# A smaller first transfer for the fold operands, and the first rounding of x moved from ScalarE to VectorE

## What is computed

```python
base = jnp.einsum('bsi,oi->bso', x, W)
low = jnp.einsum('bsi,bir->bsr', x, lora_A[labeler_index])
x = x + base + jnp.einsum('bsr,or->bso', low, lora_B_w) * 0.5
```

```python
y = irfft(rfft(x, n=1024) * rfft(K, n=1024))[..., :512] + x * D[:, None]
x = x + y * (arange(512) < length[:, None])
```

## Time and profile before

| | us |
|---|---|
| median of 3 executions | 196.37 |
| lowest and highest of them | 195.5 and 196.44 |
| the profiled execution | 195.38 |
| its span, first to last instruction | 193.3 |
| PE busy in the span | 188.3 (97%) |
| DVE, ACT, POOL busy | 125.5, 90.1, 69.9 |

### The profile page before, as it was taken

The page is one execution under the profiler, slowest core; times in us unless marked ns, Lnnn a source line. Parts: engine busy times, 40 slices in busy tenths (PEclk is TensorE's granted clock), DMA queues, the critical chain, the costliest instruction groups (busy, mean ns, idle before and its releaser), DMA issues.

```text
span 193.3 us, 2658 instructions
## 1 busy us (share of the span) xinstructions
PE 188.3 (97%) x937; PEld 157.7 (82%) x937; DVE 125.5 (65%) x163; ACT 90.1 (47%) x143; POOL 69.9 (36%) x111
## 2 busy tenths in 40 slices
PE   7799999999999999999999999999999999999994
PEld 3488887888888888888778888888999999999994
DVE  0699889369976067868006506379989777777743
ACT  2555075444339734334143221766566565565600
POOL 6048830000000377000000000279869867676700
PEclk9999999999999999999999999999999999999999
DMA  6989990000000000000001600045897988888634
GB/s 202 347 295 428 427 416 24 0 0 2 3 2 0 0 2 3 0 0 0 0 2 23 209 0 0 0 120 172 239 330 284 303 265 270 273 267 243 233 119 153
DMA packets 14654, 27.33 MB, mean 141 GB/s; under 512 B 2450, under 2 KB 4914, under 8 KB 13746
## 3 DMA queue, kind: packets, MB, share of 16 engines
q1 hardware_dynamic: 13922, 25.79, 39.0%
q10 hardware_dynamic: 720, 1.38, 2.0%
HBM read 18.69 MB, written 8.47 MB: 141 GB/s over the span
## 4 chain that ended last, share of the span: by engine, by line
PE 95%; DVE 2%; ACT 1%; issue 0%
PE y_ps L539 12%; PE y_ps L540 12%; PE y_ps L541 12%; PE k_ps L604 10%; PE k_ps L606 10%; PE k_ps L605 10%; PE low_ps L533 4%; PE low_ps L534 4%; PE low_ps L535 4%; PE y_ps L546 4%; PE y_ps L555 2%; PE y_ps L563 2%; PE y_ps L559 2%; PE low_ps L512 2%; PE k_ps L593 1%; PE k_ps L541 1%
## 5 line engine op out<-in xcount | busy, mean ns | idle before, releaser
L395 POOL TENSOR_TENSOR t_lo<-w_raw,t_hi 128x512 fp32r<-128x512 f32 x32 | 45.5, 1435 | 61.3 <-ACT t_hi L457 61.3
L741 DVE COPY_PREDICATED low_sel<-lab_mask,low_ps 32x512 f32<-32x512 int32 x32 | 23.3, 730 | 29.4 <-PE low_ps L535 28.4
L604 PE MATMUL k_ps<-xs_hi,t_hi 128*128 128x128 f32 (+3 forms) x130 | 41.6, 320 | 0.2 <-DVE x_all L813 0.2
L606 PE MATMUL k_ps<-xs_lo,t_hi 128*128 128x128 f32 (+3 forms) x130 | 41.7, 321 | 0.0
L605 PE MATMUL k_ps<-xs_hi,t_lo 128*128 128x128 f32 (+3 forms) x130 | 41.6, 320 | 0.0
L539 PE MATMUL y_ps<-x_hi,w_hi 128*128 128x512 f32 x104 | 40.6, 391 | 0.0
L541 PE MATMUL y_ps<-x_lo,w_hi 128*128 128x512 f32 x104 | 40.6, 391 | 0.0
L540 PE MATMUL y_ps<-x_hi,w_lo 128*128 128x512 f32 x104 | 40.6, 390 | 0.0
L753 DVE TENSOR_TENSOR xs_lo<-x_all,xs_hi 128x512 fp32r<-128x512 f32 x32 | 29.9, 938 | 4.7 <-ACT xs_hi L451 4.7
L813 DVE COPY_PREDICATED x_all<-len_mask,k_ps 128x512 f32<-128x512 int32 x31 | 23.2, 750 | 12.2 <-PE k_ps L606 11.9
L451 ACT CAST xs_hi<-x_all 128x512 fp32r<-128x512 f32 x32 | 19.9, 622 | 18.9 <-PE k_ps L606 18.8
(11 more groups left out here) (128 smaller groups left out, 218.7 us busy)
## 6 DMA issues: line engine op xcount, KB each, us to landing
w_raw<-k_pad SPq DMA_DIRECT2D x32, 256.0 KB, 4.3
out<-x_all SPq DMA_DIRECT2D x31, 256.0 KB, 3.6
x_all<-in_xt SPq DMA_DIRECT2D x7, 1024.0 KB, 13.9
w_raw<-in_wt ACTq DMA_DIRECT2D x4, 256.0 KB, 5.3
x_all<-in_xt SPq DMA_DIRECT2D x4, 256.0 KB, 7.4
ab_raw<-in_ab SPq DMA_DIRECT2D x1, 320.0 KB, 3.5
a_raw<-in_a_lab ACTq DMA_DIRECT2D x1, 320.0 KB, 7.2
out<-x_all SPq DMA_DIRECT2D x2, 128.0 KB, 1.7
```

Of the source, the lines that this page charges most:

```text
L395: g.tensor_tensor(t_lo[:, k % TR, :], t_raw[:, k % RAW, ::-1], f32(t_hi[:, k % TR, :]), ALU.subtract).then_inc(t_lo_done, 1)
L604: mm(o, t_hi[:, u, cols(lag)], xs_hi[:, b, x], start=(lag == 0), stop=False, skip_group_check=True)
L606: return mm(o, t_hi[:, u, cols(lag)], xs_lo[:, b, x], start=False, stop=ends, skip_group_check=True)
L741: v.copy_predicated(low_sel[:], lab_mask[rows, :].unsqueeze(1).to_broadcast([RANK, GH, P]), low_ps[rows, g % 2, :].rearrange("p (h b) -> p ...
```

## The change

- The transfer of `ab_raw` is cut in two. Rows 0 to 31 (A0 of chunk 0 and B beside it) go first; then chunk 0 of x; then rows 32 to 127; then chunks 1 to 3 of x. Each part has its semaphore.
- PE waits for the first part ahead of the first fold, and for the second part ahead of the second fold.
- The rounding of chunk 0 of x goes from ACT to DVE, between the two halves of the addition to W of chunk 0. It has a semaphore of its own (`x0_hi_done`), and the counts of `x_hi_done` are one less everywhere.
- ACT waits for both parts ahead of its use of B, much later.

```diff
-            sp.dma_start(ab_raw[:], ab).then_inc(ab_load, 16)
-            for c in range(CH):
+            sp.dma_start(ab_raw[0:RANK, :], ab[0:RANK, :]).then_inc(ab_load[0], 16)
+            sp.dma_start(x_all[:, 0:GH, cols(0)], xt[:, 0:GH, cols(0)]).then_inc(x0_load[0], 16)
+            sp.dma_start(ab_raw[RANK:P, :], ab[RANK:P, :]).then_inc(ab_load[1], 16)
+            for c in range(1, CH):
                 sp.dma_start(x_all[:, 0:GH, cols(c)], xt[:, 0:GH, cols(c)]).then_inc(x0_load[c], 16)
...
             def split_chunk_hi(c):
-                act.wait_ge(x0_load[c], 16)
-                s.copy(x_hi[:, 0:GH, cols(c)], x_all[:, 0:GH, cols(c)]).then_inc(x_hi_done, 1)
+
+                if c > 0:
+                    act.wait_ge(x0_load[c], 16)
+                    s.copy(x_hi[:, 0:GH, cols(c)], x_all[:, 0:GH, cols(c)]).then_inc(x_hi_done, 1)
...
-            act.wait_ge(ab_load, 16)
+            act.wait_ge(ab_load[0], 16)
+            act.wait_ge(ab_load[1], 16)
...
-            pe.wait_ge(ab_load, 16)
             for c in range(CH):
+                if c < 2:
+                    pe.wait_ge(ab_load[c], 16)
...
             def chunk(c):
-                pe.wait_ge(x_hi_done, c + 1)
+                if c == 0:
+                    pe.wait_ge(x0_hi_done, 1)
+                else:
+                    pe.wait_ge(x_hi_done, c)
...
-                for _, o in w_parts(c):
+                for n, o in w_parts(c):
                     v.scalar_tensor_tensor(w_raw[:, c, o], fold_ps[c][:, o], LORA_SCALING, w_raw[:, c, o],
                                            ALU.mult, ALU.add).then_inc(w_sum, 1)
-                dve.wait_ge(x_hi_done, c + 1)
+                    if n == 1:
+                        dve.wait_ge(x0_load[0], 16)
+                        v.tensor_copy(x_hi[:, 0:GH, cols(0)], x_all[:, 0:GH, cols(0)]).then_inc(x0_hi_done, 1)
+                if c == 0:
+                    dve.wait_ge(x0_hi_done, 1)
+                else:
+                    dve.wait_ge(x_hi_done, c)
```

More of the change, by code:

```diff
@@ L140, in conditioned_residual @@
         a_load = sem("a_load")
-        ab_load = sem("ab_load")
+        ab_load = [sem(f"ab_load{i}") for i in range(2)]
         idx_load = sem("idx_load")
@@ L161, in conditioned_residual @@
         masks = sem("masks")
+        x0_hi_done = sem("x0_hi_done")
         x_hi_done = sem("x_hi_done")
@@ L209, in buf_of, with hi_count, lo_count @@
             return slice(GH * (g % 2), GH * (g % 2) + GH)
-        def split_count(g):
+        def hi_count(g):
+            return CH - 1 + 2 * g
+        def lo_count(g):
             return CH + 2 * g
@@ L567, in low_group @@
             def low_group(g):
-                pe.wait_ge(x_hi_done, split_count(g))
-                pe.wait_ge(x_lo_done, split_count(g))
+                pe.wait_ge(x_hi_done, hi_count(g))
+                pe.wait_ge(x_lo_done, lo_count(g))
                 if g >= 2:
@@ L626, in _ @@
             pe.wait_ge(a_lo_done, 1)
-            pe.wait_ge(x_hi_done, CH)
+            pe.wait_ge(x_hi_done, CH - 1)
             pe.wait_ge(x_lo_done, CH)
@@ L727, in split_x_lo @@
             def split_x_lo(g, pair):
-                dve.wait_ge(x_hi_done, split_count(g - 1) + pair + 1)
+                dve.wait_ge(x_hi_done, hi_count(g - 1) + pair + 1)
                 b, h = GH * (g % 2) + 2 * pair, GH * g + 2 * pair
```

## The result

| | before | changed kernel |
|---|---|---|
| median of 6 executions, us | 196.28 | 199.09 |
| lowest and highest | 195.23 and 196.45 | 197.51 and 199.87 |
| the profiled execution, us | 195.38 | 199.87 |
| its span, us | 193.3 | 197.6 |

The medians are 2.8 us apart. The ratio on record is 1.0166, with a 95% interval of 1.0136 to 1.0196, which makes 2.7 to 3.8 us. I had forecast 0.4 us, with a range up to 197.8. The profiled execution is the slowest of the six, so its rows show more than the median loss.

What follows compares the result with a forecast made beforehand. PE was taken as the bound, busy 188.3 of 193.3 us. All terms were 0 or hidden except 0.4 us for rounding x on DVE, so the 196.37 us median became 196.8, range 195.6 to 197.8.

Steps and rivals of the forecast that it cites:

- What bounds the kernel: Whole kernel: PE, busy 188.3 of 193.3 us; the change aims at its 1.0 us wait ahead of chunk 0.
- The first part of ab alone: Start of the folds: an earlier landing hides behind PE's own queue; 0, at most 0.1 us gained.
- The first fold alone: Ahead of chunk 0: four folds run together, so one alone still ends at 6.58; 0, at most 0.1 us.
- The other three folds: Ahead of chunk 0: second part lands at 6.1, at most 6.6; folds take 1.0 us, hidden before 7.62.
- The rounding of x on DVE: Between DVE's two half sums of chunk 0: the new instruction costs 0.4 us, bounds 0.3 to 0.6.
- The tie at the low-rank product: Chunk 2's end: DVE's `a_lo` has about 0.1 us slack, so its delay makes PE lose 0.4 us.
- Rival A: Ahead of chunk 0: a late second part makes the folds hold PE; +1.5 us, 197.9 us; chance 0.10.
- Rival B: From the first fold on: PE's clock rises 2 to 3 us later; about +1.4 us, 197.8; chance 0.13.
- Rival C: Idle ahead of chunk 0: it delays the clock in timed executions; filling it gives 195.8 us; chance 0.12.
- Rival D: Start of the folds: ab's landing set it in timed executions; 0.5 us net gain, 195.9; chance 0.10.
- the sign given for D: DVE's first sum of chunk 0 starts clearly ahead of 6.5 us; also the sign for folds sharing the array.
- The number: Median of the changed kernel: likeliest 196.8 us, range 195.6 to 197.8.

Runs made afterwards that it cites:

- warm6: The kernel before with six instead of seven matmuls on the zeroed tile; 195.83 us, ratio 1.0.
- hole: The kernel before, transfers unchanged, with PE also waiting for chunk 0 of x ahead of the folds; 198.13 us, ratio 1.0119.
- x_then_whole: The kernel before with chunk 0 of x issued ahead of an uncut ab; 198.24 us, ratio 1.0154.
- cut_columns: As parts_in_row, but ab is cut by columns, each part with all 128 rows, and all folds wait for both; 196.73 us, ratio 1.0074.
- parts_in_row: The changed kernel with both parts of ab issued ahead of chunk 0 of x; 198.92 us, ratio 1.0146.
- x_on_dve: The kernel before with only the rounding of chunk 0 of x moved from ACT to DVE; 195.86 us, ratio 1.0006.
- transfers_only: The changed kernel's transfers and PE waits, with ACT rounding chunk 0 of x as in the kernel before; 199.06 us, ratio 1.018.
- filler: The changed kernel with eight matmuls on the zeroed tile between the first fold and the wait for ab's second part; 198.87 us, ratio 1.0173.
- hole_filled: As hole, with three matmuls on the zeroed tile ahead of PE's waits; 196.29 us, ratio 1.0027.
- halves: As parts_in_row, but ab is cut at row 64 and PE waits ahead of the first and third fold; 200.52 us, ratio 1.0259.
- folds_behind: The changed kernel with the folds of chunks 1 to 3 moved behind the first four matmuls of chunk 0; 198.11 us, ratio 1.015.

## Why the prediction was wrong, step by step

- **What bounds the kernel**: right. PE does, and the waits that matter are in the first 8 us.
- **The first part of ab alone, 0**: right. It landed at 3.2 us and was not waited for; warm6 shows that PE's own queue set 4.70.
- **The first fold alone, 0**: right. Alone and at the full clock it takes 1.12 us (4.33 to 5.45); in hole all four take 1.13 us (6.29 to 7.42).
- **The other three folds, "I take 6.1", bound 6.6, hidden**: this is the step that failed, a term of 0 in the sum. The part landed at 7.46, chunk 0 started 1.9 us late, and the clock added 2.3 us in the profiled execution. I had counted the bytes of SP's queue alone, while W's queue took more of the time than before, and held one more transfer worth 0.5 us at most. x_then_whole gives 6.40 for the same bytes uncut, and in cut_columns and parts_in_row one more transfer cost 1.0 us and the cut by rows another 1.2 for what is behind. The bound had come from no row on a transfer of fewer than 128 rows, and so was none. The price of the folds was short, too: a pass of 512 columns at the full clock starts 0.50 us after the one ahead of it (6.29 to 6.79 in hole's trace), not 0.43.
- **The rounding of x on DVE, c = 0.4**: the size was 0.33, within the bounds. The tie at the low-rank product is there (0.41 us idle in x_on_dve), and its cost in the median, 0.1 us (-0.4 to +0.6), leaves both 0 and 0.4 possible. In the changed kernel it is hidden altogether, since `a_lo` ends at 17.3 and the low-rank product comes near 20. Chunk 0 of x landed at 5.74, not at "about 5", just ahead of its use at 5.83.
- **Rival A, 0.10**: its mechanism is the one that happened, with the landing 0.1 us ahead of the 7.6 that it named, and a start at 9.51 instead of its 8.6. It was priced at the full clock, 1.0 us for three folds; they took 2.0.
- **Rival B, 0.13**: the clock was the other half, and its sign, starts 0.43 us apart behind 7.6, was met. Its reason stays open. In the profiled execution the clock was up ahead of the first fold, so that one can't test it; there the hole brought the clock down. In transfers_only, parts_in_row and filler it was still low behind a lone fold. I had set A and B side by side as alternatives with 0.23 between them, and one can cause the other: a late transfer opens a hole, and a hole can take the clock, as hole and hole_filled show. Together they give the +1.9 and +2.3 us of the profiled execution, which no single rival reached.
- **Rival C, 0.12**: its guess on the executions of before was right in part: the slow ones of one chip are those with a lower mean clock (196.47 to 196.67 us with 0.991). Its gain was not seen.
- **Rival D, 0.10**: DVE's first sum did start ahead of 6.5, at 5.49, the sign given for D. But the cause was the clock, which had risen before the first fold in this execution, and not the landing of ab. No time was gained.
- **The number**: the range ended at 197.8, below the median and below five of the six executions. Both parts of the loss, the later start and the clock, stood among the rivals, each with less than its size. What rival A had for it, that x competes with W, is in the bytes of both queues.

## What to carry to other kernels

A wait that moves from an engine to a transfer is as safe as the landing time, and a landing time reckoned from bytes is not safe when the transfer is cut into fewer rows: look for a row of such a transfer, or leave it whole. The cut by columns cost less here (1.2 us against 3.3 for the same cut by rows), but it cost. Where TensorE stands idle for 1 to 2 us in its first microseconds, price the clock behind the hole along with the hole; in hole it was three quarters of the cost, and three matmuls on a zeroed tile kept it. Before a new wait goes into a queue, list what stands behind it: here three folds, which DVE asked for from 7.8 us on, held up matmuls that were ready at 6.4.

## What was not expected of the hardware

- A transfer of part of the rows pulls apart the landings of what follows it in the queue: 2.4 to 2.6 us between the first and last share of chunk 0 of x (parts_in_row, halves), against 0.4 to 0.5 with all rows (before, cut_columns). It isn't the only thing that does: chunk 0 ahead of an uncut ab has 1.1 us (x_then_whole).
- The clock fell within a hole of 2.05 us (changed kernel, at 7.3), at the end of one of 1.0 us that followed one of 1.5 us (hole, at 8.4), and 1.8 us behind the end of one of 1.05 us (folds_behind, at 9.1). In before, with 1.03 us idle ahead of chunk 0 alone, the profiled execution doesn't show the lower level behind 7.6 us, but five of 23 timed ones on one chip have a mean clock below the rest.
- The rise comes at very different times in executions that start alike: at 3.9 us in the changed kernel, at 6.3 in before, and at 10.4 in filler, without an idle time in between.
- In executions where the clock is low from the start of the record, its column reads 1.00: in x_then_whole groups of four take 1.91 us at 11.4 us while the mean clock of the run is given as 1.0. In filler it reads 1.00 while the eight matmuls take 3.59 us. The time of a group of matmuls is the surer sign.
- How the 16 shares fall on engines and ports for 32, 64 and 96 rows, and so why they come apart, stays open, and so does W's part in it; the ports are argued from the Trainium skill, not shown.
